# A delta-rule stage whose decay matrices come from rows of gate sums in DRAM instead of TensorE products

## The reference

```python
mixed = silu(causal_conv1d(hidden @ w_qkv, conv_w))      # 4 taps
q, k, v = split(mixed); q, k = l2norm(q), l2norm(k)
beta = sigmoid(b); g = -exp(A_log) * softplus(a + dt_bias)
def step(St, (q_t, k_t, v_t, g_t, b_t)):                  # over 512 tokens
    St = St * exp(g_t)
    delta = (v_t - k_t @ St) * b_t
    St = St + outer(k_t, delta)
    o = q_t @ St
core = rmsnorm(o) * norm_weight * silu(z);  x = x + core @ w_out
```

## Time and profile before

| | us |
|---|---|
| median of 3 runs | 1809.51 |
| lowest and highest | 1807.46, 1811.63 |
| the profiled execution | 1807.36 |
| its span | 1805.3 |
| norm and gates | 0 to 40.0 |
| prologue of the delta stage | 40.0 to 110.1 |
| 15 full windows of 77.15 | 110.1 to 1267.3 |
| last window | 1267.3 to 1336.3 |
| the three other layers | 1336.3 to 1805.3 |

### The profile page before, as it was taken

One profiled execution on the slowest core, in us unless ns is written; L12 is line 12 of the kernel. 1 busy time (PEld: TensorE's weight loads), 2 busy tenths in 40 slices (PEclk: granted clock), 3 DMA queues, 4 the chain that ended last, 5 costly groups with the idle time before them and its releaser, 6 DMA issues. The chain is left out here.

```text
span 1805.3 us, 29318 instructions
## 1 busy us (share of the span) xinstructions
PE 1674.6 (93%) x9654; PEld 1226.7 (68%) x9654; DVE 1177.2 (65%) x2688; ACT 899.3 (50%) x2394; POOL 590.3 (33%) x893
## 2 busy tenths in 40 slices
PE   3789999999999999999999999999979989998897
PEld 2457778787777877778787777877755545555575
DVE  4468687777867778687777867778345445443445
ACT  1556657566575666657566575666221114332121
POOL 1415244242443415344242543425010012221332
PEclk9889999999999999999999999999989988769999
DMA  2010110101001010110101101000011071000413
GB/s 64 15 40 7 35 41 3 39 7 35 15 27 41 7 35 7 34 41 4 38 7 35 17 25 41 7 17 12 6 52 35 25 293 48 1 1 1 141 53 105
DMA packets 119154, 65.70 MB, mean 36 GB/s; under 512 B 91264, under 2 KB 109696, under 8 KB 118880
## 3 DMA queue, kind: packets, MB, share of 16 engines
q1 hardware_dynamic: 115664, 56.61, 11.6%
q0 software_dynamic: 2256, 6.18, 1.0%
q10 hardware_dynamic: 1088, 1.05, 0.2%
HBM read 46.19 MB, written 17.61 MB: 35 GB/s over the span
## 5 line engine op out<-in xcount | busy, mean ns | idle before, releaser
L864 DVE SCALAR_TENSOR_TENSOR dr_acc<-dr_raw,dr_wh,dr_acc 128x512 f32<-128x512 f32 x384 | 307.8, 815 | 58.3 <-ACT dr_acc L729 56.5
L1083 PE MATMUL dr_pp<-xnT,dr_wh 128*128 128x512 f32 x512 | 247.3, 617 | 6.4 <-DMA dr_wh<-in_w_head 6.0
L688 POOL TENSOR_TENSOR dr_dT<-dr_dT,cst 128x512 f32<-128x512 f32 x64 | 88.4, 1382 | 252.3 <-DVE dr_dT L898 252.3
L674 POOL TENSOR_TENSOR dr_gm<-cst,dr_hs 128x512 f32<-128x512 f32 x64 | 76.8, 1209 | 259.8 <-DVE dr_hs L858 131.9
L1083 PEld LDWEIGHTS dr_pp<-xnT,dr_wh 128*128 128x128 f32 x512 | 93.7, 195 | 92.8 <-issue 74.0
L1160 PEld LDWEIGHTS dr_pI<-dr_Y,dr_nl 128*64 128x64 f32 (+1 forms) x1536 | 125.5, 156 | 31.7 <-issue 26.7
L1177 PEld LDWEIGHTS dr_pI<-dr_V,dr_X 128*64 128x64 f32 (+1 forms) x1536 | 126.2, 156 | 28.1 <-issue 21.3
L1115 PE MATMUL dr_pp<-dr_wh,xnT 128*128 128x256 f32 x512 | 124.5, 387 | 14.9 <-ACT dr_acc L729 14.9
L1160 PE MATMUL dr_pI<-dr_Y,dr_nl 128*64 128x64 f32 (+1 forms) x1536 | 134.2, 241 | 2.1 <-DMA dr_Y<-dr_blocks_y 2.1
L1177 PE MATMUL dr_pI<-dr_V,dr_X 128*64 128x64 f32 (+1 forms) x1536 | 135.1, 242 | 0.0
L728 ACT ACTIVATE dr_raw<-dr_pp 128x512 f32<-128x512 f32 x128 | 76.2, 596 | 113.7 <-PE dr_pp L1083 90.6
(11 more groups left out here) (276 smaller groups left out, 3644.9 us busy)
## 6 DMA issues: line engine op xcount, KB each, us to landing
dr_wh<-in_w_head SPq DMA_DIRECT2D x16, 776.0 KB, 4.6
ex_w<-in_moe SPq DMA_DIRECT2D x18, 608.0 KB, 13.0
dr_wo<-in_w_out SPq DMA_DIRECT2D x16, 256.0 KB, 4.7
dr_sorted_x<-ex_zero SPq DMA_DIRECT2D x1, 3999.0 KB, 31.1
so_xt<-dr_sorted_x SPq DMA_DIRECT2D x3, 1032.0 KB, 9.6
m_w<-in_moe SPq DMA_DIRECT2D x8, 384.0 KB, 3.1
dr_blocks_l<-dr_nl SPq DMA_DIRECT2D x128, 16.0 KB, 1.7
dr_L<-dr_blocks_l SPq DMA_DIRECT2D x16, 128.0 KB, 2.0
```

What stands on the lines that cost most here:

```text
L674: pool.tensor_tensor(gm[p][:], over(k.c(C_LE), 1, U), over(hs[s][:, G_, units(c)], 2, P), ALU.mult).then_inc(s_gm[p], 1)
L688: pool.tensor_tensor(d, d, over(k.c(C_LE), 1, U), ALU.mult).then_inc(s_am, 1)
L864: dve.scalar_tensor_tensor(acc[q][:], raw[q][:, w:w + S], wh[at.ps][:, col:col + 1], acc[q][:], ALU.mult, ALU.add).then_inc(done[q], 1)
L1083: mm = pe.matmul(flat(ps), wh[at.ps][:, w0:w0 + P], k.xnT[:, kt, b * S:(b + 1) * S], start=(kt == 0), stop=(kt == KT - 1))
```

## The change

- The gates are split into a coarse part `hi` (gates floored at -120 and rounded to a grid) and a rest `lo`. The running sums of `hi` are made twice: once as tokens x heads (stored in `sc` as kind `GRID`), once turned, so that they lie as rows; these are copied and written to DRAM (`gt_rows`). The exponentials of the rest's sums are carried as kinds `BETAV` and `ELO` into the value and query scales.
- `gm`, `decay` and the bank `pG` are gone. SyncE's queue loads for each chunk the row of sums, the same 2 KB for all 128 partitions (`row`, four transfers for a window, behind `head`). GpSimd subtracts the column of sums (`gap`, first operation) and multiplies by a matrix of signs (second), in place in `dT`; `dexp` takes the exponential in place.
- `turn` and `mT` are gone. As the decay matrix now has both triangles, `mt` multiplies key products and decays straight into `nl` in the permuted column order, in three instructions, and `nl` multiplies by `cm` in place.
- `pKQ` has two banks; `gram` waits for `at` two chunks back.
- `corev` of VectorE is gone. GpSimd multiplies `o` by the gate (`oz`), and once the factor is there it multiplies by that (`corev`).
- `WINDOW` is a new order. The products that keep TensorE going in the last window (line 123) write to a bank of `pKQ`.

```diff
-G_, BETA, EGC, ESFX, ETOT = range(5)
-NKIND = 5
+GRID, BETA, BETAV, EGC, ESFX, ETOT, ELO = range(7)
+NKIND = 7
+G_FLOOR = -120.0
+G_STEP = 12288.0
...
+        self.rows_dram = nc.dram_tensor("gt_rows", [HK, CH, U * P], F32).ap()
...
+            sp.wait_ge(rows, 1)
+            sp.dma_start(k.rows_dram.rearrange("(a h) c (u j) -> (h c u) a j", a=2, u=U), sc_rows[:]
+                         ).then_inc(k.s_rows, 16)
...
-            pe.wait_ge(g_ready, 1)
-            gflat = sc[:, :, G_, :]
-            for i, m in enumerate((C_LE, C_GT, C_ONES)):
-                pe.matmul(ps_cum[i][:, 0:N].rearrange("p (h q) -> p h q", h=HK), k.c(m), gflat,
-                          start=True, stop=True).then_inc(cum, 1)
+            pe.wait_ge(split, 1)
+            for a in range(2):
+                mm = pe.matmul(ps_cum[0][:, a * P:(a + 1) * P], hi[:, a * HK // 2:(a + 1) * HK // 2], k.c(C_LE),
+                               start=True, stop=True)
+            mm.then_inc(cum, 1)
+            pe.matmul(sums(1), k.c(C_LE), hi[:], start=True, stop=True).then_inc(cum, 1)
+            pe.wait_ge(split, 2)
+            pe.matmul(sums(2), k.c(C_LE), lo[:], start=True, stop=True).then_inc(cum, 1)
+            for i, m in ((3, C_GT), (4, C_ONES)):
+                pe.matmul(sums(i), k.c(m), hi[:], start=True, stop=False)
+                pe.matmul(sums(i), k.c(C_ONES), lo[:], start=False, stop=True).then_inc(cum, 1)
...
-            for i, kind in enumerate((EGC, ESFX, ETOT)):
+            act.wait_ge(cum, 1)
+            act.activation(sc_rows[:].rearrange("p a j -> p (a j)"), ps_cum[0][:, 0:N], ACT.Copy).then_inc(rows, 1)
+            act.wait_ge(cum, 2)
+            act.activation(sc[:, :, EGC, :], sums(1), ACT.Exp).then_inc(exps, 1)
+            act.wait_ge(cum, 3)
+            act.activation(emlo[:], sums(2), ACT.Exp, scale=-1.0).then_inc(exps, 1)
+            act.activation(sc[:, :, ELO, :], sums(2), ACT.Exp).then_inc(exps, 1)
+            for i, kind in ((3, ESFX), (4, ETOT)):
                 act.wait_ge(cum, i + 1)
-                act.activation(sc[:, :, kind, :], ps_cum[i][:, 0:N].rearrange("p (h q) -> p h q", h=HK),
-                               ACT.Exp).then_inc(exps, 1)
+                act.activation(sc[:, :, kind, :], sums(i), ACT.Exp).then_inc(exps, 1)
...
+            link(spread(gs[:], g))
+            link(dve.tensor_scalar(up[:], gs[:], G_FLOOR, G_STEP, ALU.max, ALU.add))
+            dve.tensor_scalar(hi[:], up[:], -G_STEP, None, ALU.add).then_inc(split, 1)
+            dve.wait_ge(split, 1)
+            dve.scalar_tensor_tensor(lo[:], gs[:], G_FLOOR, hi[:], ALU.max, ALU.subtract).then_inc(split, 1)
             dve.wait_ge(eb_ready, 1)
             link(dve.tensor_scalar(eb1[:], eb[:], 1.0, None, ALU.add))
             link(dve.reciprocal(sg[:], eb1[:]))
-            spread(BETA, sg, beta_ready)
+            spread(sc[:, :, BETA, :], sg).then_inc(beta_ready, 1)
+            dve.wait_ge(exps, 1)
+            dve.tensor_copy(sc[:, :, GRID, :], sums(1))
+            dve.wait_ge(exps, 2)
+            dve.wait_ge(beta_ready, 1)
+            dve.tensor_tensor(sc[:, :, BETAV, :], sc[:, :, BETA, :], emlo[:], ALU.mult).then_inc(beta_ready, 1)
...
+WINDOW = """
+conv1 row0 scal conv_r1 row1 conv0 gap0 conv_r0 tapa1 tapb1 tapc1 tapa0 conv3 tapb0 gap1 v0 silu1 conv_r3 m0 row2
+tapc0 silu0 conv2 conv_r2 tapa3 dexp0 y0 tapb3 queries0 a0 qsq0 tapc3 xa0 v1 tapa2 v2 dexp1 m2 conv5 y2 row3 m1 y1
+yz tapb2 tapc2 silu3 a2 silu2 v4 keys0 xb0 gram0 conv_r5 m4 queries1 keys_r0 ksq0 a1 y4 mt0 v3 gram1 a4 solve0 qsq1
+tapa5 keys1 conv4 gap2 tapb5 xa1 mt1 dl0 at0 gap3 m3 ds0 tapc5 y3 keys_r1 at1 update0 ksq1 output0 st0 silu5 gram2
+o0 conv_r4 a3 tapa4 recall1 v5 recallq1 dexp2 rhs1 solve1 nscal tapb4 mt2 cm0 xb1 m5 cm1 square0 nl0 tapc4 dl1
+dexp3 conv6 gram3 ds1 qs1 mt3 cm2 nl1 y5 update1 silu4 output1 a5 oz0 conv7 st1 cm3 nl2 factor0 conv_r6 nl3 conv_r7
+recall2 gate3 o1 square1 rhs2 solve2 tapa7 gate_r3 vals0 dl2 corev0 ds2 vals1 recallq2 tapa6 vals_r0 tapb6 qs2
+tapb7 core0 oz1 gath factor1 vals_r1 update2 output2 tapc6 core_r0 silu6 st2 o2 project0 corev1 square2 gathr lane0
+recall3 project_r0 lane1 lane2 recallq3 core1 core_r1 gate0 rhs3 am0 solve3 lane3 lane4 factor2 qs3 lane5 project1
+dl3 output3 oz2 lane6 lane7 gate_r0 lane8 corev2 lane9 core2 project_r1 o3 oz3 lane10 gate2 lane11 core_r2 square3
+lane12 at2 gate_r2 project2 factor3 corev3 gate1 yl tapc7 putx puty project_r2 vals2 gate_r1 silu7 at3 core3
+vals_r2 vals3 am1 vals_r3 core_r3 project3 scaty am2 project_r3 scatx am3
...
-        gm = [sb(f"gm{i}", [P, U, P]) for i in range(2)]
+        rows = [sb(f"rows{i}", [P, U, P]) for i in range(2)]
         cm = [sb(f"cm{i}", [P, U, P]) for i in range(2)]
-        mT = [sb(f"mT{i}", [P, U, P]) for i in range(2)]
...
-        pG, pKQ, pA, pB = (bank(n, [P, U, P]) for n in ("pG", "pKQ", "pA", "pB"))
-        pp = [bank(f"pp{i}", [P, 4, P]) for i in range(2)]
+        pA, pB = (bank(n, [P, U, P]) for n in ("pA", "pB"))
+        pKQ = [bank(f"pKQ{i}", [P, U, P]) for i in range(2)]
...
+            def row(at, c):
+                p = c % 2
+                sp.wait_ge(k.s_rows, 16)
+                wait(sp, s_gap, 2 * (CH * at.PH + c - 2) + 1)
+                sp.dma_start(flat(rows[p]), k.rows_dram[at.PH, c].partition_broadcast(P)).then_inc(s_rows[p], 16)
...
-            run(sp, {"head": head, "gath": gath, "gathr": gathr, "putx": putx, "puty": puty, "scatx": scatx,
+            run(sp, {"head": head, "row": row, "gath": gath, "gathr": gathr, "putx": putx, "puty": puty, "scatx": scatx,
...
-            def gm_(at, c):
+                pool.tensor_tensor(rqh[s][:], rqh[s][:], c_rqh[:], ALU.mult).then_inc(s_pool, 1)
+                pool.wait_ge(s_pool, base + 9)
+                pool.tensor_tensor(rqa[s][:], rqh[s][:], rqh[s][:], ALU.mult).then_inc(s_pool, 1)
+                pool.wait_ge(s_pool, base + 10)
+                pool.tensor_tensor(rqa[s][:], rqa[s][:], c_rqa[:], ALU.mult).then_inc(s_scal, 1)
+            def gap(at, c):
                 s, p = at.ps, c % 2
                 pool.wait_ge(s_hs, at.PH + 1)
-                wait(pool, s_G, CH * at.PH + c - 1)
-                pool.tensor_tensor(gm[p][:], over(k.c(C_LE), 1, U), over(hs[s][:, G_, units(c)], 2, P),
-                                   ALU.mult).then_inc(s_gm[p], 1)
+                pool.wait_ge(s_rows[p], 16 * (2 * at.PH + c // 2 + 1))
+                wait(pool, s_O, CH * (at.H - 1) + c + 1)
+                d = dT[s][:, c]
+                pool.tensor_tensor(d, rows[p][:], over(hs[s][:, GRID, units(c)], 2, P), ALU.subtract).then_inc(s_gap, 1)
+                pool.wait_ge(s_gap, 2 * (CH * at.PH + c) + 1)
+                pool.tensor_tensor(d, d, over(k.c(C_SIGN), 1, U), ALU.mult).then_inc(s_gap, 1)
...
+            def oz(at, c):
+                s, n = at.s, CH * at.H + c
+                pool.wait_ge(s_o, n + 1)
+                taken(pool, at, [f"gate{j}" for j in (c // 2, 2 + c // 2)], 1)
+                if c:
+                    pool.wait_ge(s_full, use(at, f"core{c - 1}") + 1)
+                elif at.H:
+                    pool.wait_ge(s_full, use(at, f"core{CH - 1}", 1) + 1)
+                z = zs[s][:].rearrange("p (b c) v d -> p b c v d", b=B)[:, :, c]
+                pool.tensor_tensor(core[:].rearrange("p (b v) d -> p b v d", b=B),
+                                   o[:].rearrange("p (b v) d -> p b v d", b=B), z, ALU.mult).then_inc(s_oz, 1)
...
+            def corev(at, c):
+                m = CH * at.H + c
+                pool.wait_ge(s_fac, m + 1)
+                pool.wait_ge(s_oz, m + 1)
+                pool.tensor_tensor(core[:], core[:], over(fac[:], 2, DH), ALU.mult).then_inc(s_core, 1)
...
-                act.wait_ge(s_G, CH * at.PH + c + 1)
-                wait(act, s_O, CH * (at.H - 1) + c + 1)
-                act.activation(dT[at.ps][:, c], pG[:], ACT.Exp).then_inc(s_dt, 1)
+                act.wait_ge(s_gap, 2 * (CH * at.PH + c) + 2)
+                act.activation(dT[at.ps][:, c], dT[at.ps][:, c], ACT.Exp).then_inc(s_dt, 1)
...
-                wait(dve, s_turn[c % 2], 2 * at.PH + c // 2)
-                kk = pKQ[:].rearrange("p (b q) j -> p b q j", q=2)[:, :, 0]
-                dve.tensor_tensor(mT[c % 2][:].rearrange("p (b v) j -> p b v j", v=REP), over(kk, 2, REP),
-                                  dT[at.ps][:, c].rearrange("p (b v) j -> p b v j", v=REP), ALU.mult).then_inc(s_mt, 1)
+                wait(dve, s_Vp[c // 2], 3 * at.PH)
+                wait(dve, s_blocks, 16 * NB * at.PH)
+                kk = pKQ[c % 2][:].rearrange("p (b q) j -> p b q j", q=2)[:, :, 0]
+                d = dT[at.ps][:, c].rearrange("p (b v) j -> p b v j", v=REP)
+                to = nl[:, units(c)].rearrange("p (b v) j -> p b v j", v=REP)
+                for b0, n in ((0, 1), (1, 1), (2, 2)):
+                    of = slice(32 * b0, 32 * (b0 + n))
+                    p0 = 32 * KEPT.index(b0)
```

(42 more changed lines are left out.)

98 lines of the change are left out of this document (44 added, 54 removed).

## The result

The changed kernel takes 1706.7 us in the median of four runs (1702.1 to 1712.2), the kernel before beside it 1808.5 (1805.6 to 1811.6): a ratio of 0.944, 95% interval 0.940 to 0.948. Five more rounds, later, gave 1705.5 us and 0.942 (0.940 to 0.945). The forecast was 1731, with a range of 1707 to 1765: the kernel is 24 us faster than predicted, and the result lies just outside the range, at its lower edge.

What follows compares the result with a forecast made beforehand. TensorE's own work was taken as the bound. From the profiled 1807.4 us, 78 for 15 windows and 0.5 outside them came off, giving 1729; the median lies 2.1 above, so 1731 us, range 1707 to 1765.

Steps and rivals of the forecast that it cites:

- What bounds the kernel: In the 15 full windows: TensorE's own work makes up 75.1 of 77.15 us per window.
- TensorE's work: In each window: removing four turn (0.44 each) and four decay (0.86 each) saves TensorE 5.2 us.
- the sizing of the waits: TensorE's waits per window: 2.0 us as before, about 1.2 of it three bank turns at the end; bounds 0 and 4 to 5.
- The second rival: In the windows: almost no TensorE waits, 69.95 to 70.6 us per window, 1700 to 1711 us in all; chance 0.07.
- GpSimd: In each window: GpSimd's work rises from 30.7 to 45.3 us of some 72 and does not become the bound.
- The contention: VectorE beside GpSimd in each window: 3.0 us lost for 17.6 of large GpSimd work, in proportion 5.5 for 32.2.
- The fourth rival: In the windows: VectorE, slowed beside GpSimd, becomes the bound and the kernel slower; chance 0.05, another 0.01 between.
- Rows: Loads of gate sums in each window: the first lands about 7 us in or less, costing TensorE nothing.
- the slack of "4 to 5 us": Between the rows' use in gap and dexp and TensorE's keys0 and gram0: about 4 to 5 us left.
- The third rival: In the windows: rows or GpSimd's queue come late, TensorE waits 4 to 7 us per window, 1754 to 1805 us; chance 0.12.
- Gates' phase: Before the delta stage: 256-column products at 0.98 us each and small VectorE steps add 4.5 us, bounds 2 and 6.
- Prologue and last window: Around the 15 windows: the prologue 4 us shorter (bounds -8 and +3), the last window 1 us shorter.

Runs made afterwards that it cites:

- e4: The changed kernel with one unused 512-column product and four unused transposes per chunk added on TensorE: 1783.3 us, ratio 0.987 to the kernel before.
- e7: The changed kernel in the stage list of before, with dexp0 moved behind conv_r2: 1828.9 us, ratio 1.011 to the kernel before.
- e1: The changed kernel in the stage list of before, without decay and turn, row and gap where gm stood: 1920.1 us, ratio 1.064 to the kernel before.
- e3: The kernel before with conv7 and gate2, and conv_r7 and gate_r2, swapped in its list: 1798.4 us, ratio 0.996 to it unswapped.
- e9: The changed kernel with the output stage's multiply by the factor on VectorE instead of GpSimd: 1784.7 us, ratio 0.984 to the kernel before.
- e6: The changed kernel with two more 128x512 GpSimd multiplies in each chunk's oz stage: 1880.5 us, ratio 1.039 to the kernel before.

## Why the prediction was wrong, point by point

**What bounds the kernel: right.** TensorE's own work; e4 puts 5.4 us a window back at full price.

**TensorE's work: right.** Predicted 5.2 us less for a window, measured 75.17 - 69.72 = 5.45; distances between starts were the right price. Over 15 windows the difference is 3.7 us.

**The step that failed** is the sizing of the waits: "With some small ones elsewhere I take 2.0, as before". They measured 0.76, and 0.4 of it is a bank turn; three bank turns, "about 1.2 us", had been expected. 15 x 1.24 = 18.6 us, most of the error of 27 against the profiled run. (The rest, in us: TensorE's work 3.7, the gates' phase 5.1, prologue 1.8, last window 2.7, and -4.8 from the later stages.)

What the runs show in its place is that most of the 2.0 us belonged to the old list and not to the kernel. (The prediction puts them down to short transposes; the largest is `gate1`'s.) The two waits for banks stay at 0.88 and 0.35 us in the old list with VectorE relieved (e7, and e1 likewise), and two swaps in that list take the larger one away with VectorE as it was (e3). The new list has its own condition: VectorE's queue must be short at the window's end. With one multiply back in it, a wait of 3.2 us for `project_r2` appears (e9). So the order removed the waits, and the relief of VectorE allowed this order; I had kept a number of the old list for a kernel with a new one. The second rival, 1700 to 1711, had this mechanism and the right time, and got 0.07. "Against it: the bank turns remain" was true and small: 0.4 us.

**The list had no term beyond its waits.** The changed code in the old list takes 1920 us, 1829 with one stage moved, and the kernel before in the new list 1980. What a carefully made old order could reach with the new content is open; these runs show only how much depends on the two being fitted to each other.

**GpSimd: right in its effect, low in size.** Predicted 45.3 us for a window, measured 50.4. `gap`'s first operation takes 1.16 instead of 1.05, `ds` 1.32 instead of 1.05, and `oz` 1.51 instead of 1.38. The contention grew faster than in proportion: the taps pay 24 x (0.926 - 0.74) = 4.5 us, 1.8 before, for GpSimd's large work of 35.3 us (17.6 before). VectorE has 59.9 where 57.6 was predicted; 0.8 of this is `nl`, which now reads both operands from SBUF and takes 0.88 instead of 0.68, a term that the prediction left out. The fourth rival did not come. One reason is that many of VectorE's operations read PSUM and keep their time beside GpSimd: `project_r2` takes 0.68 in the changed kernel though `corev` begins on GpSimd in the middle of it (rows above), and `at` 0.68 in the mean of 12 windows, before and after.

Multiply and tap in e9 last 1.73 and 1.75 beside `am`. Each begins while a GpSimd operation has some 1.2 us to go, and 1.2 + 0.7 is 1.9. The Trainium skill (SBUF — State Buffer, section "SBUF: two separate sides") states of a VectorE operation with two SBUF inputs and a GpSimd operation that reads SBUF that whichever starts first holds the shared port pair for its whole instruction, and the other waits. The two durations agree with that roughly. Over a window the loss is far from one for one, 4.5 us on the taps for 35.3.

**Rows: right by luck.** `gap0` begins 9.7 us into the window, not 7: the first row is asked for 0.7 us later than reckoned (3.2), and takes 6.4 us to land beside the weights, not 4.7. No wait of PE comes of it. But the slack of "4 to 5 us" was not there. ScalarE waits 1.60 us at `dexp1`, and behind it come a table load of 1.28 us and two silus. The silu of the keys ends at 616.59, `keys0` begins at 617.07: half a microsecond.

```profile
606.98 1.10 POOL L717 TENSOR_TENSOR dr_dT<-dr_rows,dr_hs 128x512 f32<-128x512 f32 x1 [9.53 <-issue]
...
612.72 0.63 ACT L845 ACTIVATE dr_dT<-dr_dT 128x512 f32<-128x512 f32 x1 [1.60 <-POOL dr_dT L719]
613.37 1.28 ACT L803 ACT_TABLE_LOAD   x1
614.66 0.63 ACT L803 ACTIVATE dr_kq<-dr_acc 128x512 f32<-128x512 f32 x1
...
615.96 0.63 ACT L803 ACTIVATE dr_kq<-dr_acc 128x512 f32<-128x512 f32 x1
...
617.07 0.66 PE L1153 MATMUL dr_pp<-cst,dr_kq 128*128 128x128 f32 x4
```

The third rival was nearer than its 0.12 says. e1 shows how it looks when it comes.

**Gates' phase: predicted +4.5, measured -0.6.** From the first VectorE operation on PSUM (26.21 before, 22.51 after) to the end it is 13.82 before, 16.96 after: +3.1, of which the 256-column products have about 0.86, later 0.43 each, not 0.98. What hid this cost is no work of the change: 32 unchanged products ahead of it took 7.06 us before and 3.75 after.

```profile
18.72 3.75 PE L244 MATMUL gt_ps_ab<-w_ab,xnT 128*128 128x64 f32 x32 [0.94 <-PEq L134]
...
36.09 1.06 PE L257 MATMUL gt_ps_cum<-gt_hi,cst 128*128 128x256 f32 x2
36.94 0.99 PE L258 MATMUL gt_ps_cum<-gt_lo,cst 128*128 128x256 f32 x2
37.77 0.60 PE L257 MATMUL gt_ps_cum<-gt_hi,cst 128*128 128x256 f32 x2
```

**Prologue and last window** gave 1.8 and 2.7 us more than predicted. In the last window PE's wait for the last `core` shrank from 3.46 to 2.19. The chain did not get quicker: from the start of the last `o` to that `core` it is 5.15 us before and 5.43 after, and behind the factor the multiply takes 1.04 on GpSimd and took 1.14 on VectorE. PE has `project2` to do meanwhile, which before began ahead of that `o`. The later stages, which nothing touches, took 4.8 more.

## What to carry to other kernels

Before you keep a wait "as before" in a kernel with a hand-written list, ask whether it belongs to the work or to the order. Here it belonged to the order, and the new order could drop it only because an operation had left the queue of its releaser. Busy shares of 70% say nothing about room in a chain that feeds the bound: of 10.8 us of added GpSimd work in e6, 8.2 came back as idle time of TensorE. And long waits cost more than their length, since the granted clock is lower behind some of them. Content and order are one change: the new list with the output multiplies, or all of the content, of before ran 98 and 273 us above the two together, the new content in the old list 213, and 122 with one stage moved.

## What was unexpected of the hardware

The same 32 products of the gates' phase, at the same place, take from 3.75 to 7.06 us, by run. In four runs it is 3.75 or 3.76 us, at a granted clock of 1.00. In four it is 4.6 to 4.9, with 0.74 to 0.80 recorded for these microseconds, which roughly accounts for them. In six, the kernel before among them, it is 7.06, nearly twice 3.75 as at the lower level, and yet the record has 1.00. Why is open. It is an offset of up to 3.3 us from a part that no edit touched.

The twelve products behind the delta stage do likewise: 5.39 us at a granted clock of 1.00 in nine runs, 7.0 to 7.6 at 0.70 to 0.77 in five. What follows tends to go the other way: the time from their start to the end of the span was 471.1 to 476.1 in the nine, and 468.6 to 470.8 in four of the five (474.2 in the fifth). In part this is the clock again: the 32 products of the router right behind them took 3.71 us at 1.00 before and 4.47 at 0.81 after. The rest is open.
